# Causal attention stage: the mask moves from a TensorE seed to a VectorE addition, the maxima are taken off on GpSimd, and the denominators are shuffled one step earlier

## The reference, cut to what matters

```
q = (queries @ Wq + bq).reshape(B, L, H, dk)      # 16 heads of 16
k = (keys @ Wk + bk)...; v = (values @ Wv + bv)...
scores = einsum('blhd,bshd->bhls', q, k)
causal = triu(ones((L, S)), k=1)
scores = where(causal, -inf, scores)
attn = softmax(scores * scale, axis=-1)
out = einsum('bhls,bshd->blhd', attn, v) @ Wo + bo
```

## Time and profile before

| what | value |
|---|---|
| median of three runs | 1714.85 us (1712.42 to 1718.21) |
| the profiled execution | 1716.57 us, its span 1714.6 us |
| TensorE matmul busy | 1568.2 us, 91% of the span |
| TensorE weight loads busy | 1024.7 us, 60% |
| VectorE busy | 892.1 us, 52% |
| ScalarE busy | 812.9 us, 47% |
| GpSimd busy | 371.5 us, 22% |

### The profile page before, as it was taken

The page is one execution under the profiler, slowest core; times in us unless marked ns, Lnnn a source line. Parts: engine busy times, 40 slices in busy tenths (PEclk is TensorE's granted clock), DMA queues, the critical chain, the costliest instruction groups (busy, mean ns, idle before and its releaser), DMA issues. The chain is left out here.

```text
span 1714.6 us, 34568 instructions
## 1 busy us (share of the span) xinstructions
PE 1568.2 (91%) x13646; PEld 1024.7 (60%) x13646; DVE 892.1 (52%) x1863; ACT 812.9 (47%) x1585; POOL 371.5 (22%) x337
## 2 busy tenths in 40 slices
PE   8899999999799999999799999999787899899965
PEld 3455555555356666656565999999344666566642
DVE  4566666511555565555242211111273889667758
ACT  4355555533144544455431222222254788556666
POOL 0012222221100010000028300000721777311222
PEclk9999999999899999999789999999999899999988
DMA  7000000010200000000043799997379443000001
GB/s 264 1 1 2 1 1 2 22 34 1 85 20 11 20 20 20 20 11 2 14 162 126 227 328 329 326 326 238 94 193 219 118 95 88 12 12 12 2 1 44
DMA packets 148051, 150.16 MB, mean 88 GB/s; under 512 B 69890, under 2 KB 135106, under 8 KB 147890
## 3 DMA queue, kind: packets, MB, share of 16 engines
q1 hardware_dynamic: 144818, 140.60, 26.9%
q0 software_dynamic: 3072, 7.34, 1.4%
HBM read 120.40 MB, written 27.53 MB: 86 GB/s over the span
## 5 line engine op out<-in xcount | busy, mean ns | idle before, releaser
L2506 DVE TENSOR_TENSOR masked<-masked 128x512 f32<-128x512 f32 x70 | 49.8, 712 | 200.9 <-ACT masked L2408 200.9
L958 DVE CUSTOM_DVE_ANT_0 x_unused<-psum,masked 112x439 f32<-112x439 f32 x256 | 141.8, 610 | 20.3 <-PE psum L781 19.6
L896 ACT ACTIVATE x_probs<-psum,key_mask 125x448 f32<-125x448 f32 x192 | 106.1, 635 | 77.4 <-PE psum L801 77.4
L2349 PEld LDWEIGHTS psum<-mix_xb,mix_up 128*128 128x128 f32 x1120 | 130.6, 192 | 2.1 <-issue 0.4
L2349 PE MATMUL psum<-mix_xb,mix_up 128*128 128x128 f32 x1120 | 130.7, 275 | 0.0
L2359 PE MATMUL psum<-mix_down,masked 128*128 128x256 f32 x560 | 127.0, 380 | 0.1
L1477 PE MATMUL psum<-fold_full,hT 128*112 128x512 f32 x256 | 113.8, 597 | 1.3 <-DVE fold_part L1872 1.3
L2359 PEld LDWEIGHTS psum<-mix_down,masked 128*128 128x128 f32 x560 | 103.5, 190 | 13.4 <-DVE masked L2506 0.4
L1721 ACT COPY masked<-psum 112x448 f32<-112x448 f32 x128 | 63.8, 530 | 60.6 <-PE psum L1508 60.3
L781 PE MATMUL psum<-x_kT,x_qz 32*112 32x439 f32 x512 | 88.4, 591 | 3.2 <-DVE x_kT L943 3.2
L2408 ACT ACTIVATE masked<-psum 128x512 f32<-128x512 f32 x70 | 41.8, 597 | 97.1 <-PE psum L2349 97.1
(11 more groups left out here) (338 smaller groups left out, 3277.5 us busy)
## 6 DMA issues: line engine op xcount, KB each, us to landing
mix_up<-in_moe_up SPq DMA_DIRECT2D x35, 1024.0 KB
mix_down<-in_moe_down SPq DMA_DIRECT2D x35, 1024.0 KB
offset_rows<-join_rows SPq DMA_DIRECT2D x16, 784.0 KB, 5.7
hrow<-offset_rows SPq DMA_DIRECT2D x16, 784.0 KB, 5.2
x_ctx<-in_ctxT SPq DMA_DIRECT2D x16, 375.0 KB, 3.1
slots_x<-masked SPq DMA_DIRECT2D x1, 4480.0 KB, 21.4
mix_rows<-slots_x SPq DMA_DIRECT2D x35, 128.0 KB, 3.4
slots_y<-mix_result SPq DMA_DIRECT2D x35, 128.0 KB, 3.5
```

What stands on the lines that cost most here:

```text
L896: nc.scalar.activation(probs[0:rows, 4 * (c % 2) + r], psum[0:rows, bank("tile", n, 4 * c + r), 0:G].rearrange("p (k t) -> p k t", k=4), A ...
L958: nc.vector.tensor_tensor_reduce(unused[:, at], psum[0:T, at, 0:KEYS], masked[0:T, n * KEYS:(n + 1) * KEYS], -1.0, -3.0 * NEG, ALU.add, AL ...
L2349: mm = nc.tensor.matmul(psum[:, 2 * u + half, m * BLOCK:(m + 1) * BLOCK], e_up[:, w, c, (half * H4 + m) * P:(half * H4 + m + 1) * P], xb[: ...
L2506: nc.vector.tensor_tensor(e_hidden[:, u, half * H4:(half + 1) * H4], e_relu[:, half], e_relu[:, half], ALU.mult).then_inc(hidden_ready.sem, 1)
```

## The change: what it does

For the causal stage alone (the other two keep their instructions):

- TensorE no longer seeds the banks with the mask. The score matmuls start the accumulation themselves.
- VectorE has a new add_mask(n, r): scores from PSUM plus the 112 x 112 mask, broadcast over the four heads, written to SBUF. It counts on a new semaphore, masked. shift is gone. largest now reads the SBUF tile and gives negated maxima.
- VectorE's order is add_mask 0, add_mask 1, largest 0, add_mask 2, largest 1, add_mask 3, largest 2, largest 3, then centre, take_values(n), and now spread_denominators(n-1) instead of spread_denominators(n-2) behind group 0.
- GpSimd adds the negated maxima, four move(n, r) behind normalise(n-2), counted on moved.
- ScalarE waits on moved for each exps, runs exps 0 and 1, copy_mix(n-1), exps 2 and 3, take_keys, and then take_logs(n-1) and invert(n-1), ahead of the square. The logs and inverses no longer stand between and behind the copies.
- TensorE waits on masked in place of shifted before it overwrites a bank.

```diff
-        banks_free = factored if offset else shifted
+        banks_free = factored if offset else masked if causal else shifted
@@ scores
-                    if not offset:
+                    if future:
                         nc.tensor.matmul(psum[0:T, r, 0:G], identb[0:T, 0:T], maskb[:], start=True, stop=False, skip_group_check=True)
...
-                        mm = nc.tensor.matmul(..., start=offset, stop=True, skip_group_check=not offset)
+                        mm = nc.tensor.matmul(..., start=not future, stop=True, skip_group_check=future)
@@ turned weights behind the stage
-                        pe.wait_ge(*shifted.after(At(NB - 1), 2 * (n - NB) + k))
+                        pe.wait_ge(*masked.after(At(NB - 1), 2 * (n - NB) + k))
@@ exps
-                act.wait_ge(*(moved.after(At(n), r - 2) if offset else shifted.after(At(n), r)))
+                act.wait_ge(*(moved.after(At(n), r - 2 if offset else r) if not future else shifted.after(At(n), r)))
@@ ScalarE loop
-                if last and not offset and n <= NB:
+                if last and future and n <= NB:
                     take_logs(n - 2)
...
-                if last and not offset and n <= NB:
+                if last and future and n <= NB:
                     invert(n - 2)
...
                 if now and not offset:
-                    for r in range(NG):
+                    for r in range(NG if future else 2):
                         exps(n, r)
...
-                if now and offset:
+                if now and not future:
                     for r in range(2, NG):
                         exps(n, r)
...
-                if offset and before and n < NB:
+                if not future and before and n < NB:
                     take_logs(n - 1)
                     invert(n - 1)
@@ VectorE
             def largest(n, r):
                 x, mx, src = block_of(n, r)
-                if offset:
...
+                if not future:
+                    if causal:
+                        dve.wait_ge(*masked.after(At(n), r))
+                        dve.wait_ge(*moved.after(At(n - 2), r))
...
                     nc.vector.tensor_reduce(mx, x, X, ALU.max, negate=True).then_inc(maxed.sem, 1)
...
+            def add_mask(n, r):
+
+                x, _, src = block_of(n, r)
+                dve.wait_ge(*scored.after(At(n), r))
+                dve.wait_ge(*tile_turned.after(At(n - 2), NG - 1))
+                nc.vector.tensor_tensor(x, src, const["maskf"].unsqueeze(1).broadcast_to([T, HG, T]), ALU.add).then_inc(masked.sem, 1)
@@ VectorE loop
                 elif now and causal:
+                    add_mask(n, 0)
                     for r in range(NG):
+                        if r + 1 < NG:
+                            add_mask(n, r + 1)
                         largest(n, r)
-                        shift(n, r)
-                        if r == 0 and last:
-                            spread_denominators(n - 2)
                     beside.dve_centre(dve, n, 6)
                     take_values(n)
+                    if before:
+                        spread_denominators(n - 1)
@@ GpSimd
             def move(n, r):
                 pool.wait_ge(*maxed.after(At(n), r))
+                if causal:
+                    pool.wait_ge(*masked.after(At(n), r))
                 x = probs[:, n % 2, HG * r:HG * (r + 1)]
                 nc.gpsimd.tensor_tensor(x, x, rowmax[...].unsqueeze(2).broadcast_to([T, HG, T]), ALU.add).then_inc(moved.sem, 1)
...
                 if n >= 2:
                     normalise(n - 2)
+                if n < NB and causal:
+                    for r in range(NG):
+                        move(n, r)
```

More of the change, by code:

```diff
@@ L1381, in token_attention @@
             qz, ctx, ctx_loaded = cross.qz, cross.ctx, cross.ctx_loaded
+            masked, moved = s.counter("masked", NG), s.counter("moved", NG)
         if offset:
@@ L1498, in scores @@
                         q = qz_all[rows, e, m, n * T:(n + 1) * T] if offset else qz[rows, g % 2, e, m, t:t + T]
-                        mm = nc.tensor.matmul(psum[0:T, r, k * T:(k + 1) * T], q, kT[rows, g % 2, m, t:t + T], start=offset, stop=True, skip_group_check=not offset)
+                        mm = nc.tensor.matmul(psum[0:T, r, k * T:(k + 1) * T], q, kT[rows, g % 2, m, t:t + T], start=not future, stop=True, skip_group_check=future)
                         if k == 3:
@@ L1810, in _ @@
         def _(dve):
-            for x in (maxed, shifted, added) + ((q_read,) if not causal else ()) + ((cross.q_read,) if offset else ()) + ((v_read,) if not future else (qk_made, fscored, fmaxed, combined, centred, fsummed, fmixed)) + ((factored, biased_here) if offset else ()) + (spread,):
+            for x in (maxed, added) + ((shifted,) if future else (masked,) if causal else ()) + ((q_read,) if not causal else ()) + ((cross.q_read,) if offset else ()) + ((v_read,) if not future else (qk_made, fscored, fmaxed, combined, centred, fsummed, fmixed)) + ((factored, biased_here) if offset else ()) + (spread,):
                 x.start(dve)
@@ L1859, in largest @@
                 x, mx, src = block_of(n, r)
-                if offset:
-                    dve.wait_ge(*(biased_here.after(At(n), r) if r < 2 else biased.after(At(n), r - 2)))
-                    dve.wait_ge(*exped.after(At(n - 2), r))
+                if not future:
+                    if causal:
+                        dve.wait_ge(*masked.after(At(n), r))
+                        dve.wait_ge(*moved.after(At(n - 2), r))
+                    else:
+                        dve.wait_ge(*(biased_here.after(At(n), r) if r < 2 else biased.after(At(n), r - 2)))
+                        dve.wait_ge(*exped.after(At(n - 2), r))
                     nc.vector.tensor_reduce(mx, x, X, ALU.max, negate=True).then_inc(maxed.sem, 1)
@@ L1869, in shift @@
                 x, mx, src = block_of(n, r)
-                dve.wait_ge(*(combined.after(At(n)) if future else maxed.after(At(n), r)))
+                dve.wait_ge(*combined.after(At(n)))
                 dve.wait_ge(*tile_turned.after(At(n - 2), NG - 1))
                 nc.vector.tensor_tensor(x, src, mx.unsqueeze(2).broadcast_to([T, NG, T]), ALU.subtract).then_inc(shifted.sem, 1)
+            def add_mask(n, r):
[3 more added lines that the diff above has]
+                nc.vector.tensor_tensor(x, src, const["maskf"].unsqueeze(1).broadcast_to([T, HG, T]), ALU.add).then_inc(masked.sem, 1)
             def combine(n):
@@ L1996, in _ @@
                         take_cross_queries(1, 0)
-                    else:
+                    elif future:
                         spread_denominators(n - 2)
```

## The result

The changed kernel takes 1708.33 us, the median of 20 runs (1702.97 to 1716.87); the kernel before took 1716.60 us in 20 runs beside them (1711.71 to 1726.62). The ratio is 0.9946, 95% interval 0.9933 to 0.9959: 9.3 us less, between 7.0 and 11.5. Two later comparisons on other chips gave 0.9939 and 0.9936, 10.5 and 11.0 us less.

A forecast was written before the change was run, and what follows sets the result against it. The prediction took TensorE to set the causal stage's pace. Seeds 13.8, ScalarE's order 2.1 and the centre 1.6, less 5.4 of losses, gave 12.1 us won: 1714.85 to 1702.8, put as 1703, range 1697.5 to 1709.

The forecast's parts named there:

- the granted clock in the stage is no longer 1.00: Causal stage: TensorE's granted clock below 1.00, listed among the signs that the forecast is wrong; no size or chance given.
- the rival of ScalarE's tail: Even steps 2 to 14: last exps and log end 0.5 to 1 us late, taking 3.5 to 7 us; 1708; chance 0.19.
- everything hidden: Causal stage: ScalarE catches up and none of the losses is real; 17.5 us gained, 1697; chance 0.13.
- Seeds, 0.86 each: TensorE's list: a batch's mask seeds hold it for 0.86 us; 16 batches give 13.8 us won.
- The rival in which it sets the pace: GpSimd: moves of about 1.5 us make it the stage's clock, about 18 us lost against 17.5 gained; chance 0.04.
- The lock: Steps 1, 8, 12: VectorE's scale collides with GpSimd's moves; taken as 0, at most 3.0 us, 1706; chance 0.03.
- Step 9, 0.4 lost: Steps 8 to 9: ScalarE's list of 7.8 us exceeds the 7.4 us wanted between copies; 0.4 us lost.
- Steps 12 and 13, 1.9 lost: ScalarE's list of 7.8 us against 5.9 wanted between copies; 1.9 us lost, the largest single loss.
- Step 3, 0.5 lost: Step 3 on ScalarE: the keys' copy stands ahead of the log; 0.5 us lost.
- Start, 2.0 lost: Steps 0 to 2: variance waits in step 1 and held copies in step 2; 2.0 us lost in all.
- The centre's wait in step 15, 1.6 won: Step 15: the norm's centre comes earlier on VectorE, so the output's 1.65 us wait shrinks; 1.6 us won.
- ScalarE's part: ScalarE's copies: log and inverse no longer delay them, so TensorE's waits go; 2.1 us won, between 1.1 and 3.4.

The follow-up runs named there:

- e2: Changed kernel plus spare matmuls (fillers) where TensorE waits in steps 1, 3 and 13; 1706.37 us, 0.9923 of the kernel before.
- e9: Changed kernel, log and inverse of batches 1 and 11 deferred to the middle of steps 3 and 13, fillers in steps 1 and 3; 0.9923 of the kernel before.
- e4: Kernel before with the causal stage's mask seeds left out and nothing in their place; 1712.43 us, 0.9951 of the kernel before.
- e5: Changed kernel with the causal stage's four mask seeds put back; 1705.20 us, 0.9978 of the kernel before.
- e1: Changed kernel as it is, a second profile; 1708.40 us, 0.9939 of the kernel before.
- e11: Changed kernel as it is, a third profile; 1705.83 us, 0.9936 of the kernel before.
- e6: Changed kernel with spare matmuls (fillers) in step 1 alone; 1696.55 us, 0.9929 of the kernel before.
- e10: Changed kernel with spare matmuls (fillers) in steps 3 and 13 alone; 1706.13 us, 0.9929 of the kernel before.
- e12: Changed kernel with fillers in step 1 alone, as e6, a second profile; 1705.96 us, 0.9930 of the kernel before.
- e13: Second run of e9, with deferred log and inverse and fillers in steps 1 and 3; 1705.37 us, 0.9923 of the kernel before.
- e3: Changed kernel with ScalarE's log and inverse put back between and behind the copies; 1732.13 us, 1.0076 of the kernel before.

## Why the prediction was right, point by point

The direction, the range and the mechanism held: TensorE set the pace, and its list got shorter. With the clock held (e2) the stage is 160.24 - 147.43 = 12.8 us shorter, where the sum said 12.1. What the prediction lacked is a term for the clock: it named "the granted clock in the stage is no longer 1.00" as what would make it wrong, and gave it no chance and no price. That sign came. In three profiles of the changed kernel the term was 7.5, 7.5 and 1.5 us. In the medians it may be the 2 to 4 us between the 9.3 to 11.0 won and the 13.2 of e2 and e9, but intervals that overlap don't show that.

The range held narrowly, and the gain of 9.3 us is just under the 9.5 to 15 that the forecast stood for. The time is the one that the rival of ScalarE's tail had (1708), yet not by its mechanism: that tail was to lengthen every even step, and those of batches 2, 4, 6 and 10 take 7.24 or 7.25 us each, less than the forecast's own 7.39. Nor was everything hidden, which would have been 17.5 us.

- *Seeds, 0.86 each.* Over-sized: 0.76 in a regular step by e4 and e5, 12.2 us for 16 batches and not 13.8. The distance from the first seed to the scores isn't what the list loses with them. Even steps still went from 8.18 to 7.24 us, since the new order gives 0.18 in each, a part of ScalarE's 2.1 us that the 7.39 left out. The losses below are counted against 0.86, as forecast.
- *VectorE.* Predicted eight operations in 4.4 us; in step 0 they run from 1491.95 to 1496.26, 4.3.
- *GpSimd.* Predicted 933 ns a move, measured 934. The rival in which it sets the pace is out.
- *The lock.* Taken as 0; it was 0.65 us, on the path, in the first two profiles. Scale (L285) took 1.73 us in step 2 of the changed kernel's first profile and 1.72 in that of e1, 0.65 above its 1.08. It met normalise, which the prediction hadn't considered, and not the moves, in a step that began late by a fall in step 1. The late mask additions, moves and exps behind it made the keys' copy late, and TensorE's wait for that in step 3 is 1.12 us, shown above:

```profile
1510.30 1.14 POOL L2055 TENSOR_TENSOR qz_all<-qz_all 128x448 f32<-128x448 f32 x1 [5.79 <-ACT qz_all L1717]
...
1510.66 1.73 DVE L285 TENSOR_TENSOR hT<-hT,sq 128x896 f32<-128x896 f32 x1
```

  In e11 scale starts first, and it is normalise that takes longer, 1.88 us in place of 1.14, at no cost to the stage; the wait in step 3 is 0.48 us:

```profile
1502.70 1.07 DVE L285 TENSOR_TENSOR hT<-hT,sq 128x896 f32<-128x896 f32 x1
1502.91 1.88 POOL L2055 TENSOR_TENSOR qz_all<-qz_all 128x448 f32<-128x448 f32 x1 [4.83 <-ACT qz_all L1717]
...
1510.57 0.60 PE L1509 MATMUL psum<-ident,second_result 112*112 112x112 f32 x4 [0.48 <-ACT gateT L1677]
```

  The profiles of e2, e5, e6, e9, e10, e12 and e13 have it as e11. By that rule of the Trainium skill ("SBUF — State Buffer", "Who interferes with whom") the collision was possible, and the trace agrees; its price was 0.65 us, not 3.0.
- *Step 9, 0.4 lost.* Wrong, nothing was: 9 to 10 went from 11.80 to 10.27, and steps 8 and 9 together won 2.28 us, two times 0.86 and 0.56.
- *Steps 12 and 13, 1.9 lost.* Over-sized. From the scores of 12 to those of 14 it took 17.04 us before and 16.10 now at full clock (5.80 and 10.30), 0.9 less where two seeds are 1.7: 0.8 lost. The first copies are 7.34 us apart and not 7.8, because exps that find their moves done follow each other in 0.52 us. The wait itself is there as forecast, 1.86 us:

```profile
1604.19 0.96 ACT L1722 COPY masked<-psum 112x448 f32<-112x448 f32 x2 [1.99 <-PE psum L1509]
...
1611.05 0.58 ACT L1717 ACTIVATE qz_all<-qz_all 128x448 f32<-128x448 f32 x1
...
1611.53 0.95 ACT L1722 COPY masked<-psum 112x448 f32<-112x448 f32 x2
...
1612.19 0.57 PE L1509 MATMUL psum<-ident,second_result 112*112 112x112 f32 x4 [1.86 <-ACT masked L1722]
```

- *Step 3, 0.5 lost.* Under-sized. 3 to 4 went from 11.22 to 11.62 at full clock, 1.3 lost: besides the late copy, turn 1 waits for the keys' copy, which stands behind the exps (0.99 and 0.48 us in e11).
- *Start, 2.0 lost.* Over-sized: to the scores of batch 3, 24.62 us before (25.48 with the first seeds) and 22.62 in e2. That is 2.9 won of 3.4 for four seeds and 0.6 for the copy, 1.1 lost.
- *The centre's wait in step 15, 1.6 won.* Missed. From the last scores to the end 20.85 us became 20.72. The wait for the centre is gone, but what TensorE does ahead of the output ends 0.9 us later, 0.53 of it a wait of the average for GpSimd's half sum, which stood behind the moves of batch 14. So the output came 0.8 us earlier, and a wait of 0.82 us of the variance for its pair sum took most of that back: that sum waited for the square, which now stands behind ScalarE's last exps, log and inverse. The prediction gave neither a price there. With the seeds kept (e5) the end takes 19.83 us.
- *ScalarE's part* was priced as 2.1 won against later losses. e3 shows that its larger worth was to have the inverse ready before GpSimd's list reaches normalise; without it the change is a loss of 13 us.

The errors of the single terms went both ways and mostly cancelled: too much for the seeds, the centre and the losses of the start and of steps 9, 12 and 13, too little for step 3 and nothing for scale. That the sum came so close at full clock is in part luck. (The prediction's "1.1 us twice" is a slip: the earlier trace rows has 1.1 for two waits together, and its sum uses 0.56 each.)

## What to carry to other kernels

When work leaves the engine that sets the pace, price the waits that take its place twice: once as idle time and once as a lower clock, which here cost 3.0 us behind 1.5 us of waits (step 3 of e12), in some executions and not in others. Filler matmuls in known waits held the clock in all 11 cases here; where the wait has gone they stand in the way themselves, as in step 1 of e6, and their gain in the median time is within the noise. And when an in-order engine gets a new job, look at what it already has queued ahead: move that one's inputs earlier first, as the inverse here, or the new job waits behind the old.

## What the runs showed of the hardware that I had not expected

- The same instruction stream with the same waits loses TensorE's full clock in one execution and keeps it in the next (fillers in step 1 alone, steps 3 and 13: 11.61 and 10.29 us in e6, 14.66 and 11.84 in e12). One profile of such a kernel isn't enough.
- While the clock is low, steps don't simply take longer by its share: a fall in step 0 cost 1.5 us there and was won back entirely in step 1 of e10, where another engine was the limit; one in step 3 cost 3.0 us, all on the path (14.66 us in e12, 11.62 in e11).
- When VectorE's scale (two SBUF inputs) and GpSimd's normalise overlap, the one that starts second takes about 0.7 us longer: scale 1.73 us beside a normalise of 1.14 that began 0.36 us before it, or normalise 1.88 beside a scale of 1.07 that began 0.21 before. Only the longer scale reached TensorE.
